# A subtraction handed from VectorE to GpSimd, and GpSimd's features one outer product ahead, in a linear-attention decoder block

## What is computed

```python
q = feature_map(x @ wq + bq); k = feature_map(x @ wk + bk); v = x @ wv + bv
# feature_map(x) = where(x > 0, x + 1, exp(x))
S = S + einsum('bhd,bhe->bhde', kt, vt)          # running sums over the 64 steps
z = z + kt
num = einsum('bhd,bhde->bhe', qt, S);  den = einsum('bhd,bhd->bh', qt, z) + 1e-6
x = x + (num / den) @ wo + bo
```

## Time and profile before

| | |
|---|---|
| median of 3 runs | 619.33 us |
| time of the profiled execution | 620.77 us |
| its span, first to last instruction | 619.0 us |
| mean granted TensorE clock | 0.975 |
| busy: PE, DVE, ACT, POOL | 554.9, 503.6, 395.7, 410.3 us |
| the 128 statistics of the attention's slots, first and last | 3.6 and 258.1 us |

### The profile page before, as it was taken

How to read it: one execution, slowest core, us unless ns; L and a number is a source line. 1 busy time by engine, 2 the same in 40 slices (tenths; PEclk the granted TensorE clock), 3 DMA queues, 4 the chain that set the end, 5 groups by cost and what they waited for, 6 DMA issues and landing times.

```text
span 619.0 us, 16196 instructions
## 1 busy us (share of the span) xinstructions
PE 554.9 (90%) x4286; PEld 410.2 (66%) x4287; DVE 503.6 (81%) x1416; ACT 395.7 (64%) x1070; POOL 410.3 (66%) x475
## 2 busy tenths in 40 slices
PE   2888999999999998787998868999999999999993
PEld 1343444444444454465997535899999999999993
DVE  4499999999999999765487898466887878877883
ACT  3556777767666775423877412445888888878882
POOL 2999888888888985204876402764576766757762
PEclk9999999999999998989899887999999999999997
DMA  5510111111161111832566570221111111111110
GB/s 154 176 64 1 35 36 35 34 47 46 43 102 35 35 35 34 123 105 70 171 189 171 101 115 10 60 46 38 37 50 50 48 49 48 52 39 48 52 45 23
DMA packets 49976, 41.03 MB, mean 66 GB/s; under 512 B 21971, under 2 KB 40278, under 8 KB 49926
## 3 DMA queue, kind: packets, MB, share of 16 engines
q1 hardware_dynamic: 44150, 29.68, 19.8%
q0 software_dynamic: 4960, 10.49, 6.6%
q10 hardware_dynamic: 816, 0.26, 0.2%
HBM read 27.54 MB, written 12.88 MB: 65 GB/s over the span
## 4 chain that ended last, share of the span: by engine, by line
PE 54%; DVE 16%; issue 14%; DMA 5%; ACT 5%; POOL 4%; DVEq 1%; SPq 1%; POOLq 0%; ACTq 0%
PE bank L1351 28%; PE run L1351 22%; DVE st L884 3%; DVE R L908 3%; PE run L1618 2%; DMA w_s<-gram_d 2%; PE bank L1355 2%; ACT xs L788 2%; POOL qk L560 1%; DVE mean_early L1059 1%; DMA ct<-in_ctx_r 1%; ACT xh L685 1%; PE run L1542 1%; POOL shared L569 1%; DVE zq L924 1%
## 5 line engine op out<-in xcount | busy, mean ns | idle before, releaser
L569 POOL TENSOR_TENSOR shared<-v,qk 128x1024 f32<-128x1024 f32 x64 | 125.0, 1953 | 7.5 <-POOL qk L560 5.7
L624 POOL DMA_INDIRECT shared<-xs_d,row_u x91 | 87.7, 963 | 62.3 <-DVE row_u L1249 31.3
L631 POOL DMA_INDIRECT out_x<-shared x64 | 63.6, 994 | 47.6 <-DVE shared L1321 20.8
L908 DVE TENSOR_TENSOR R<-run,qk 128x1024 f32<-128x1024 f32 x64 | 77.7, 1215 | 10.5 <-PE run L1351 9.9
L918 DVE TENSOR_REDUCE num<-R 128x128 f32<-128x1024 f32 x64 | 77.7, 1213 | 1.5
L1351 PE MATMUL bank<-wqkv,xT 128*64 128x128 f32 (+1 forms) x384 | 69.9, 350 | 5.2 <-ACT v L667 4.5
L1351 PEld LDWEIGHTS bank<-wqkv,xT 128*64 128x64 f32 (+1 forms) x384 | 33.1, 158 | 59.0 <-issue 30.1
L1351 PE MATMUL run<-shared,tris_s 64*64 64x512 f32 x512 | 70.6, 622 | 0.1
L817 ACT ACTIVATE shared<-run,scale_s 128x128 f32<-128x128 f32 (+1 forms) x78 | 30.1, 386 | 41.2 <-PE run L1618 41.2
L685 ACT ACTIVATE xh<-X,nb,rs 128x128 f32 (+1 forms) x126 | 52.0, 502 | 4.4 <-POOL nb L551 4.4
L560 POOL TENSOR_TENSOR qk<-ex,rl 128x256 f32<-128x256 f32 x64 | 46.6, 728 | 9.1 <-ACT ex L669 6.9
(11 more groups left out here) (271 smaller groups left out, 1417.0 us busy)
## 6 DMA issues: line engine op xcount, KB each, us to landing
xs_d<-xs SPq DMA_DIRECT2D x16, 270.0 KB, 5.4
X<-in_x SPq DMA_DIRECT2D x16, 256.0 KB, 2.8
ct<-in_ctx_t SPq DMA_DIRECT2D x16, 256.0 KB, 2.9
ct<-in_ctx_r SPq DMA_DIRECT2D x16, 256.0 KB, 3.7
gram_d<-gd SPq DMA_DIRECT2D x14, 256.0 KB, 2.4
w_s<-in_w_experts SPq DMA_DIRECT2D x8, 384.0 KB, 3.9
circ<-prob_d SPq DMA_DIRECT2D x30, 64.0 KB, 2.8
shared<-xs_d,row_u POOLq DMA_INDIRECT x91, 2.6
```

Of the source, the lines that this page charges most:

```text
L569: nc.gpsimd.tensor_tensor(outer[k].rearrange("p (h e d) -> p h e d", h=H, e=D), vv.unsqueeze(3).broadcast_to([P, H, D, D]), kk.unsqueeze(2 ...
L624: nc.gpsimd.indirect_dma_start(xg[q], None, xs_d[:, :], bass.IndirectOffsetOnAxis(ap=rows, axis=0)).then_inc(xg_in[q], 16)
L631: nc.gpsimd.indirect_dma_start(out[:, :], bass.IndirectOffsetOnAxis(ap=xg[(NXI + j) % NX][:, DEST:DEST + 1].bitcast(U32), axis=0), yg[q], ...
L908: nc.vector.tensor_tensor(R[:, 0:D * E].rearrange("p (h e d) -> p h e d", h=H, e=D), run[k % 2][:].rearrange("p (h e d) -> p h e d", h=H, ...
```

## The change

Four edits, all in the attention's slots. The subtraction `df` goes from DVE's `moments` to a new POOL function `differences`, with a semaphore `m_df` of its own; it is issued between O(2) and O(3), and ACT's `deviations` and DVE's `stats` wait for it. The sum `mv` becomes a reduction with one input. DVE issues `key_dots` before the statistics of group n+3 instead of behind them. POOL's order becomes F(0), shifts, F(1), O(0), F(2), O(1), F(3), O(2), differences, O(3). The parts below are, in order, of POOL (new function, slot), of ACT and of DVE (two functions, slot).

```diff
+            def differences(at, p, own, seen):
+
+                pool.wait_ge(m_st, seen)
+                need(pool, m_sq, 2 * (at + 2))
+                nc.gpsimd.tensor_tensor(df[p][:, own, :, 0], st[:, own, :, 1], st[:, own, :, 4], ALU.subtract).then_inc(m_df, 1)
...
             def slot(n, i):
-                m, a1 = moment_slot(n, i, -1), stage(n, i, 1)
+                m, now, a1 = moment_slot(n, i, -1), moment_slot(n, i, 0), stage(n, i, 1)
...
                 if m:
                     shifts(*m)
                 if a1:
-                    outer_product(*a1, 0)
                     for k in range(1, GT):
                         features(*a1, k)
-                        outer_product(*a1, k)
+                        outer_product(*a1, k - 1)
+                if now:
+                    differences(*now, stats_before(n + 1, i))
+                if a1:
+                    outer_product(*a1, GT - 1)
...
             def deviations(at, p, own):
 
-                act.wait_ge(m_mv, 2 * (at + 3) + 2)
+                act.wait_ge(m_df, at + 4)
+                act.wait_ge(m_mv, at + 4)
                 need(act, m_ve, at + 3)
...
             def stats(g, at, h):
-                need(dve, m_mv, 2 * (at + 3))
+                need(dve, m_mv, at + 3)
+                need(dve, m_df, at + 3)
...
-                nc.vector.tensor_tensor(df[p][:, own, :, 0], st[:, own, :, 1], st[:, own, :, 4], ALU.subtract).then_inc(m_mv, 1)
-                nc.vector.tensor_tensor(mv[p][:, own], st[:, own, :, 1:3], st[:, own, :, 4:6], ALU.add).then_inc(m_mv, 1)
+                halves = st[:, own].rearrange("p s t (h f) -> p s t f h", h=2)[:, :, :, 1:3]
+                nc.vector.tensor_reduce(mv[p][:, own], halves, AX.X, ALU.add).then_inc(m_mv, 1)
...
                 if c:
                     quotients(*c)
+                if b:
+                    key_dots(*b)
                 if z:
                     g, p, r = z
                     dve.wait_ge(x_in[p], 16 * r + 16)
                     stats(g, m[0], 0)
-                if b:
-                    key_dots(*b)
```

More of the change, by code:

```diff
@@ L252, in build @@
         ct_in = sems("ct_in", 2)
-        m_st, m_mv, m_sq, m_ve, m_rs, m_mr, m_nb, a_xh = (sem(n) for n in ("m_st", "m_mv", "m_sq", "m_ve", "m_rs", "m_mr", "m_nb", "a_xh"))
+        m_st, m_mv, m_df, m_sq, m_ve, m_rs, m_mr, m_nb, a_xh = (sem(n) for n in ("m_st", "m_mv", "m_df", "m_sq", "m_ve", "m_rs", "m_mr", "m_nb", "a_xh"))
         a_ex = sem("a_ex")
```

## The result

The changed kernel takes 632.97 us (median of 4 runs, 632.14 to 633.58), the kernel before, run beside it, 619.5. The ratio is 1.0216, 95% interval 1.0198 to 1.0234: slower by 2.2%, some 13.5 us. The prediction had 640.3, with 628 to 658 as its range.

What follows compares the result with a forecast made beforehand. DVE, PE and POOL were taken as nearly full, 14.45 us a slot; afterwards the ring through D binds. 22.9 + 3.1 - 5.0 = 21 later: 620.77 gives 641.8, less 1.4 is 640.3 us; range 628 to 658.

Steps and rivals of the forecast that it cites:

- POOL's work alone: POOL's attention slot without lateness: 13.39 us, 1.06 below 14.45, with D, the moved subtraction, at 0.20.
- The gap at V: POOL idles at F(2), F(3) while V(k) on ACT awaits O(k-2): 0.92 to 1.09 us in loop, about 0.75 written out.
- The wait on D and its ring: ACT's deviations await POOL's subtraction D, delaying tile 0, P(1), E(1), F(1): period 16.1 us in loop, 15.4 written out.
- The sum's end: Last group: F(1) 22.9 us later, O(1) 3.1 more, less 5.0 to spare: S(1) 21 later.
- Faster: Rival: V's wait is met early, so DVE gives back its 6.5 us stall: 613 us, chance 0.06.
- POOL's own chain alone: Rival: only POOL's chain binds, 15.3 us a loop slot, 14.95 written out, deviations hidden: 631 us, chance 0.22.
- The clock: Rival: PE idles 1.9 us ahead of P(1), its clock falls: 665 us, or 653 in half the slots; chance 0.19.

Runs made afterwards that it cites:

- Run 1: Kernel before with only POOL's new order of features and outer products; subtraction, sum and dots stay on VectorE: 625.13 us, ratio 1.0116.
- run 4: Changed kernel with four buffers of v8 in place of two: 622.17 us, ratio 1.0065 to the kernel before.
- run 3: Changed kernel with ACT's deviations issued behind tile 0's evacuations, not ahead of them: 628.45 us, ratio 1.0157 to the kernel before.
- run 2: Changed kernel with the old order of features and outer products, the subtraction ahead of O(3): 612.01 us, ratio 0.9892 to the kernel before.
- run 5: Changed kernel with four buffers of v8 and ACT's deviations behind tile 0's evacuations: 622.81 us, ratio 1.0062 to the kernel before.
- run 9: Kernel of run 5 with POOL's shifts issued ahead of F(0): 615.63 us, ratio 0.9952 to the kernel before.
- run 7: Kernel before with key_dots ahead of the statistics as the only edit: 619.6 us, ratio 0.9994.
- run 10: Kernel of run 2 with POOL's shifts issued ahead of F(0): 614.11 us, ratio 0.9925 to the kernel before.

## Why the prediction was right, step by step

*POOL's work alone, 1.06 less a slot.* Right: the three waits of 0.24 went, D costs 0.21 and lies back to back with O(2) and O(3). The slot of 15.55 less the features' three waits is 13.29, where 13.39 was forecast.

*The gap at V.* Right in place and nearly in size: 0.86 measured in the loop and 0.69 written out, against 0.92 to 1.09 and 0.75. The unknown in it, POOL's signal to ACT, was bounded by 0.08 and 0.25; it is 0.03 (O(1) ends at 160.58, V(3) starts at 160.61), under the lower bound, which was ACT's signal to POOL. Run 1 shows the new order alone to cost 1.2%, with this gap in it (at F(2) 0.91, since ACT's norm waited for nb ahead of tile 2), and run 4 that without V's wait the changed kernel is 1.5% faster.

*The wait on D and its ring.* Right, shown by run 3: it binds, and 0.6% goes with it. The term was mis-sized: 15.52 against 16.1. By parts, F(1) to D's end is 9.80 (forecast 9.99), D to the first Relu 0.24 (0.33), Relu to E(1)'s end 5.19 (5.33), E(1) to F(1) 0.25 (0.25): 15.48, 0.42 under the 15.90 worked out, and choosing the middle towards 16.41 added 0.2. Over the loop's eight slots that is some 5 of the 8 us by which S(1) of the last group came sooner than forecast. The written-out slots took 14.97 where 15.4 was forecast (246.20 - 231.24 = 14.96), the first period 13.81 (32.26 - 18.45) where 14.95 was, some 3.7 together.

*The sum's end.* F(1) of the last group came 14.7 later (246.20 - 231.53), forecast 22.9; the part behind it, 3.1 more for O(1) less 5.0 of lead, came out as -1.8 (12.9 - 14.7). So up to there the whole miss lies in the periods.

*The rivals.* Faster: the stall did go, and run 2 puts it at 1.1%, but the order took it away. POOL's own chain alone: by the time this rival did better than the forecast. Its 631 is 2 from the result, the forecast's 640.3 is 7, and its 15 periods of 227.1 in all are nearly the 227.75 measured; the result lies in the range because the range was stretched to 628 for this rival. Its mechanism does not hold: F(1) would not wait, and it does, 0.54 in the loop; with the wait on D out of the way run 3 has 15.18 a slot, not 15.52. The sum agrees by luck, a loop slot 0.2 longer than the rival's 15.3 against a first period 1.1 shorter. The ring lies only 0.3 above the chain, where the forecast had 0.8, and that is the size that it had wrong. The clock did not fall in the slots (1.00): the idle stretch of 1.9 ahead of P(1) came as two, 0.49 ahead of P(0) and 0.92 ahead of P(1), because P(0) waits for `xT`, which on ACT stands behind V(3) as well; the prediction overlooked that.

*What it missed.* The ring through nb. It lay below the other two in the changed kernel, where the norm in the loop shows no wait for nb, but it is why undoing both foreseen obstacles (run 5) did not bring the gain.

## What to carry to other kernels

Before moving an instruction ahead of the one that hides its input's latency, follow the input back through the producer's queue: here the feature's exponential stood behind a copy that waited for the very outer product just issued. When an engine's work is handed to another in the middle of a full slot, ask what queue the consumer of the result stands in, since a wait at the head of an in-order queue holds up everything behind it. And where several rings have nearly the same length, opening one gives only the distance to the next (15.5, 15.2, 14.9, 14.3 a slot in the changed kernel and runs 3, 5 and 9). Here the old order, in which none of these rings binds (run 2, 13.9), came out ahead of each repair of the new one (of run 9 by 0.6%, with intervals that touch).

## What was not expected of the hardware

A VectorE subtraction of two inputs in SBUF, 8 values a row, took from 0.16 to 1.70 us in one execution (run 7). In the kernel before, 11 of the 12 wide ones ended 0.02 to 0.04 behind the GpSimd addition then running, as in the earlier trace rows. That does not hold beside every GpSimd instruction: at 15.81 the subtraction, there 4 values a row, took 0.17 while the root's power ran on to 16.12. The sum beside it, as a reduction with one input, took 0.16 to 0.18 in every slot of the changed kernel, and no more where it ran inside an outer product, as in run 10 at 162.71.
